# Edge sums of a graph network: the ring of gathered edge tiles with 32 places for 16, and rings of eight groups for emptied banks and first rows

## What is computed

```python
def reference(x, src, dst, ...):
    # L0: out = segment_sum(mlp(concat(x[src], x[dst])) * edge_weight, dst)
    # L1: agg = segment_sum(h[src], dst);  mean = agg / max(deg, 1)      (twice)
    # L2: out = segment_sum(h[src] * dinv[src] * dinv[dst], dst)         (twice, self loops too)
    # L3: out = segment_sum(v[src] * softmax_by_source(scores), dst)
    x = _layernorm(x + L0(x)); x = _layernorm(x + L1(x))
    x = _layernorm(x + L2(x)); x = _layernorm(x + L3(x))
```

## Time and profile before

| | us |
|---|---|
| runs | 8763.08, 8755.55, 8756.22 |
| median | 8756.22 |
| profiled execution, its own time | 8752.19 |
| its span, first to last instruction | 8750.5 |
| mean granted TensorE clock | 0.724 |

### The profile page before, as it was taken

How to read it: one execution, slowest core, us unless ns; L and a number is a source line. 1 busy time by engine, 2 the same in 40 slices (tenths; PEclk the granted TensorE clock), 3 DMA queues, 4 the chain that set the end, 5 groups by cost and what they waited for, 6 DMA issues and landing times. The chain is left out here.

```text
span 8750.5 us, 136064 instructions
## 1 busy us (share of the span) xinstructions
PE 5075.0 (58%) x26949; PEld 3942.2 (45%) x26950; DVE 4064.5 (46%) x13584; ACT 2826.8 (32%) x6967; POOL 4235.5 (48%) x4934
## 2 busy tenths in 40 slices
PE   3666667705679556965785567544444444414577
PEld 2555444504568445854564455333322233303555
DVE  3555558861222122755662227544444444452458
ACT  0544452361343124841331248311111111100239
POOL 4777750056630565036615664555555555507650
PEclk7766679955789567976896679666666666655679
DMA  1222225572358223943574458311111111122348
GB/s 31 65 66 66 67 60 173 183 242 64 93 156 248 70 85 116 337 161 101 156 230 120 118 169 288 117 49 53 47 48 49 48 48 48 48 20 61 90 149 295
DMA packets 610422, 1013.48 MB, mean 116 GB/s; under 512 B 174962, under 2 KB 177296, under 8 KB 610064
## 3 DMA queue, kind: packets, MB, share of 16 engines
q1 hardware_dynamic: 279472, 417.77, 16.1%
q10 hardware_dynamic: 197568, 359.75, 11.6%
q0 software_dynamic: 133280, 234.88, 10.9%
HBM read 648.88 MB, written 363.07 MB: 116 GB/s over the span
## 5 line engine op out<-in xcount | busy, mean ns | idle before, releaser
L447 PE MATMUL agg_bank<-agg_msgs,agg_onehot 128*128 x7840 | 1573.5, 361 | 976.0 <-issue 697.9
L447 PEld LDWEIGHTS agg_bank<-agg_msgs,agg_onehot 128*128 128x128 f32 x7840 | 1344.7, 256 | 1273.3 <-issue 1263.5
L385 DVE TENSOR_TENSOR agg_onehot<-iota,rel 128x512 f32<-128x512 f32 x1176 | 814.3, 692 | 1717.5 <-issue 630.3
L316 POOL DMA_INDIRECT agg_msgs<-y,agg_rows x784 | 784.3, 1000 | 409.3 <-issue 210.9
L1446 PE MATMUL score_look<-score_rounded,score_loT 128*128 128x392 bf16 x392 | 178.5, 455 | 716.9 <-ACT score_loT L1515 535.1
L1398 POOL DMA_INDIRECT by_source<-score_line,score_places x392 | 397.3, 1013 | 261.7 <-DVE score_line L1572 152.7
L482 ACT ACTIVATE agg_kept<-agg_bank,inv_root 128x128 f32<-128x128 f32 x784 | 226.5, 367 | 879.9 <-PE agg_bank L447 453.5
L1093 POOL DMA_INDIRECT mlp_xs<-in_x,mlp_rows x392 | 396.6, 1012 | 233.5 <-issue 152.0
L482 ACT ACTIVATE agg_kept<-agg_bank,inv_deg 128x128 f32<-128x128 f32 x784 | 224.2, 368 | 875.2 <-PE agg_bank L447 665.4
L447 PE MATMUL agg_bank<-agg_weighted,agg_onehot 128*128 x1568 | 349.5, 394 | 265.4 <-DVE agg_onehot L385 137.5
L313 POOL DMA_INDIRECT agg_weight<-weights,agg_rows x392 | 408.9, 1043 | 182.2 <-issue 111.5
(11 more groups left out here) (333 smaller groups left out, 12898.8 us busy)
## 6 DMA issues: line engine op xcount, KB each, us to landing
sums<-agg_kept ACTq DMA_DIRECT2D x588, 256.0 KB
agg_first<-y ACTq DMA_DIRECT2D x196, 256.0 KB
messages<-mlp_m SPq DMA_DIRECT2D x98, 256.0 KB
agg_first<-in_x ACTq DMA_DIRECT2D x98, 256.0 KB
agg_msgs<-messages SPq DMA_DIRECT2D x98, 256.0 KB
l_z<-sums SPq DMA_DIRECT2D x98, 256.0 KB
x<-l_o POOLq DMA_DIRECT2D x98, 256.0 KB
l1a_s<-sums SPq DMA_DIRECT2D x98, 256.0 KB
```

The source lines that it names most:

```text
L316: pool.indirect_dma_start(msgs[:, j, :], None, table[:, :], bass.IndirectOffsetOnAxis(ap=rows[:, third, j:j + 1], axis=0)).then_inc(sm[f"g ...
L385: nc.vector.tensor_tensor(onehot[:, j, :, :], k.iota[:, 0:P].unsqueeze(1).to_broadcast([P, Q, P]), k.rel[:, ds(i * (4 * Q) + j * Q, Q)].un ...
L447: t.matmul(bank[:, column[q], :], onehot[:, j, q, :], messages[:, slot[q], :], start=False, stop=True, skip_group_check=True)\
```

## The change

`RING` becomes 32, and a new constant `KEPT` = 8 sizes the rings `kept` and `first` and their semaphores, while the PSUM banks stay `BANKS` = 4. ScalarE's loop now goes over eight groups; a bank number is taken modulo 4. A bank emptied for group g is refilled for group g+4, now from place (u+4) modulo 8 of `first`, and that place is then loaded for group g+12 (before, g+8). SyncE's loop in agg0 and agg5 goes over eight groups instead of four. GpSimd's loops cover three blocks of 32 gathers.

```diff
-RING = 16
+RING = 32
 BANKS = 4
+KEPT = 8
...
-    ROUNDS = (GROUPS - 2 * BANKS) // BANKS
+    ROUNDS = (GROUPS - BANKS - KEPT) // KEPT
...
-        kept = sb("kept", [P, BANKS, Q, C])
+        kept = sb("kept", [P, KEPT, Q, C])
...
-            first = sb("first", [P, BANKS, Q, C])
+            first = sb("first", [P, KEPT, Q, C])
...
-                        if live(i, u):
+                        if live(i, u, RING // Q):
                             load(i, u)
-                        if weights is not None and live(*before_by(i, u, 2)):
-                            arrive(*before_by(i, u, 2))
-
-                    rounds(sp, body, 2 if weights is not None else 0)
+                        if weights is not None and live(*before_by(i, u, 2, RING // Q), RING // Q):
+                            arrive(*before_by(i, u, 2, RING // Q))
+
+                    rounds(sp, body, 2 if weights is not None else 0, deep=RING // Q)
...
-                    to = bank[:, u * Q:(u + 1) * Q, :]
+                    to = bank[:, u % BANKS * Q:(u % BANKS + 1) * Q, :]
...
-                    g = i * BANKS + u
+                    g = i * KEPT + u
+                    b = u % BANKS
...
+                    after_it = (u + BANKS) % KEPT
                     if not last_round or g + BANKS < GROUPS:
-                        fill(u, i + 2)
+                        fill(after_it, i + (1 if after_it > u else 2))
                     act.dma_start(rows_of(out, g), kept[:, u, :, :]).then_inc(sm[f"written{u}"], 16)
-                    if before is not None and (not last_round or g + 2 * BANKS < GROUPS):
+                    if before is not None and (not last_round or g + BANKS + KEPT < GROUPS):
                         act.wait_ge(sm["ready"], g + (BANKS + 1))
-                        load_first(g + 2 * BANKS, u)
+                        load_first(g + (BANKS + KEPT), after_it)
```

More of the change, by code:

```diff
@@ L261, in aggregate @@
     BLOCKS, REST = ET // RING, ET % RING
-    ROUNDS = (GROUPS - 2 * BANKS) // BANKS
+    ROUNDS = (GROUPS - BANKS - KEPT) // KEPT
     whole = rows_of_edges is None or weights is not None
     loads = RING // Q if whole else RING
-    sm = phase(nc, name, [f"gathered{j}" for j in range(loads)] + [f"written{u}" for u in range(BANKS)] + [f"before{u}" for u in range(BANKS)]
+    sm = phase(nc, name, [f"gathered{j}" for j in range(loads)] + [f"{s}{u}" for s in ("written", "before") for u in range(KEPT)]
                + [f"weight{u}" for u in range(RING // Q)] + ["rows", "pass_pool", "pass_dve", "arrived", "hot", "tallied", "tally_c", "tally_to_act", "tally_rooted", "tally_to_pe", "tally_offset", "onehot", "summed", "zeros", "cleared", "ready", "emptied", "weighted"])
@@ L481, in empty @@
                         if scale is not None:
-                            last = a.activation(kept[:, u, q, :], bank[:, u * Q + q, :], ACT.Copy, scale=scale[:, ds(g * Q + q, 1)])
+                            last = a.activation(kept[:, u, q, :], bank[:, b * Q + q, :], ACT.Copy, scale=scale[:, ds(g * Q + q, 1)])
                         elif q == 0:
-                            last = a.activation(kept[:, u, :, :], bank[:, u * Q:(u + 1) * Q, :], ACT.Copy)
+                            last = a.activation(kept[:, u, :, :], bank[:, b * Q:(b + 1) * Q, :], ACT.Copy)
                     last.then_inc(sm["emptied"], 1)
                     act.wait_ge(sm["emptied"], g + 1)
+                    after_it = (u + BANKS) % KEPT
                     if not last_round or g + BANKS < GROUPS:
-                        fill(u, i + 2)
+                        fill(after_it, i + (1 if after_it > u else 2))
                     act.dma_start(rows_of(out, g), kept[:, u, :, :]).then_inc(sm[f"written{u}"], 16)
-                    if before is not None and (not last_round or g + 2 * BANKS < GROUPS):
+                    if before is not None and (not last_round or g + BANKS + KEPT < GROUPS):
                         act.wait_ge(sm["ready"], g + (BANKS + 1))
-                        load_first(g + 2 * BANKS, u)
+                        load_first(g + (BANKS + KEPT), after_it)
                 if before is not None:
-                    for u in range(BANKS):
+                    for u in range(KEPT):
                         load_first(u, u)
@@ L504, in _ @@
                         act.wait_ge(sm["ready"], u + 1)
-                        load_first(u + BANKS, u)
-                for u in range(BANKS):
+                        load_first(u + KEPT, u)
+                for u in range(KEPT):
                     empty(0, u, False)
                 with act.Fori(1, ROUNDS) as i:
-                    for u in range(BANKS):
+                    for u in range(KEPT):
                         empty(i, u, False)
-                for g in range(ROUNDS * BANKS, GROUPS):
-                    empty(g // BANKS, g % BANKS, True)
+                for g in range(ROUNDS * KEPT, GROUPS):
+                    empty(g // KEPT, g % KEPT, True)
                 if tally is not None and tally[0] is k.dst_lo:
@@ L515, in _ @@
                     a.activation(k.root[:, :], k.inv_root[:, :], ACT.Sqrt).then_inc(sm["tally_rooted"], 1)
-                for u in range(BANKS):
-                    act.wait_ge(sm[f"written{u}"], 16 * len(range(u, GROUPS, BANKS)))
+                for u in range(KEPT):
+                    act.wait_ge(sm[f"written{u}"], 16 * len(range(u, GROUPS, KEPT)))
         end_phase(nc, sm)
```

## The result

The changed kernel took 8855.73 us (median of 4 runs, 8847.41 to 8865.14), the kernel before 8755.88 us on the same chip (4 runs, 8748.25 to 8763.08). The ratio is 1.0107, with a 95% interval of 1.0095 to 1.0120: 1.1% slower, and 5.7 us above the range that was forecast. The profiled execution took 8857.90 us, its span 8856.3 us, the mean granted TensorE clock 0.729 (before 0.724).

A forecast was written before the change was run, and what follows sets the result against it. It took gather phases to be bound by one account shared by gathers and other engines' instructions. Five phases at +8.7 us, all else 0, gave +44 us on 8752.19, 8796; plus 4.0 to the median, 8800 us, range 8735 to 8850.

The forecast's parts named there:

- the lag: End of each gather phase: GpSimd finishes further ahead, leaving more quads after the last gather; 8.7 us per phase, 44 in all.
- The slow stretch: Gather phases: SyncE, VectorE and TensorE step at 0.7 us until the full ring pauses GpSimd; expected fewer and longer, 20 us and more.
- the 12 to 20: Sign in the later profile: 12 to 20 one-hots remain after the last gather, instead of 7 to 9.
- agg0, `kept` and `first`, and the fewer turns: Phase without gathers, rings of eight and half as many loop turns: each taken as 0, with small possible effects.
- The first rival: Gather phases: slow stretches come at their own times, so 32 places outlast them; -250 us, 8506 us, chance 10%.
- The account: Gather phases: gathers and other engines' instructions draw on one always-spent time budget, 1.218 us per GpSimd count, 0.0202 per other count.
- still fills each window: Sign in the later profile: prices 1.218 and 0.0202 us times the counts still use up each window's time.
- I take half, 6 quads or 8.7 us per phase: End of each gather phase: 6 more quads after the last gather, between 0 and 12; 44 us over five phases.
- the full lag: Ring full at each last gather: 12 quads of 1.45 us, 17.4 us per phase, +87 us, 8843 us; up to 8864.
- The net price of a quad: Each quad done after the last gather instead of before: 1.85 us less 0.4 given back, 1.45 us.
- The gross price: Time per quad after the last gather, averaged over the earlier profile's five phase ends: 1.85 us.
- The end of a phase is not covered by anything: End of each gather phase: work left when GpSimd finishes has no gathers beside it; cost taken as 8.7 us per phase.

The follow-up runs named there:

- depth 16 in the ring of 32: The changed kernel with its 32 places, loops and buffers, but GpSimd allowed only 16 tiles ahead of TensorE; 8766.57 us, ratio 0.9998 to the kernel before.
- the lead taken back early: The changed kernel with GpSimd allowed 32 tiles ahead for the first 74 groups of gathers, 16 for the last 24; 8834.53 us, ratio 1.0081 to the kernel before.
- the added instructions: The kernel before with four unread semaphore increments behind each count in SyncE's loop in agg1 to agg4; 8829.71 us, ratio 1.0075.

## Why the prediction was wrong, and where it was right

The direction and the mechanism of the lag held; its size did not, and the time fell 5.7 us above the range.

**What held.** The ring's waits were moved, not removed: 463 us of idleness against 479. The slow stretch lasted until the larger ring was full, and its end followed the pause. First to last gather changed by -0.4 to -0.8%, and 18 to 20 one-hots were left, within the 12 to 20 that were named as the sign. GpSimd's waits at the ring in agg1 are fewer and longer only before 2300 (22 of 51.4 us, the longest 7.6, against 29 of 59.0, the longest 4.5), not behind it. agg0, `kept` and `first`, and the fewer turns were put at 0, and the 0.9992 of the ring of 16 with rings of eight and the 0.9998 of depth 16 in the ring of 32 bear that out. The first rival, ring waits that come back as time, had no part in it.

**The account.** It was named as a sign, "still fills each window", and held only roughly. Windows of agg1 after come to 94 to 96 us of 100. From first to last gather of agg1 it gives 416 x 1.218 + 3634 x 0.0202 = 580 us before and 404 x 1.218 + 3417 x 0.0202 = 561 after, 19 us less, where 2.4 us less were measured. Twelve of the counts that are gone are short row copies; charged per gather, at 1.218 x 416/392 = 1.293 us, it gives 580 and 576 for 591.3 and 588.9. Two more rows of the kernel before speak against it as a general rule, agg3 from its first to its last gather, and a window in L0's edge phase:

```profile
3821.30:4425.70 604.40, 375.05 (x1870) 277.14 (x1868) 343.53 (x935) 160.26 (x453) 400.06 (x415) 0.73 0.41 123
...
500.00:600.00 100.00, 70.16 (x350) 54.36 (x349) 55.83 (x226) 53.83 (x148) 72.08 (x86) 0.70 0.24 69
```

The windows at 2000 and 4220 were the two it was solved from, so agg3 never tested it: there 5126 counts of the others stand beside the gathers, against 3634 in agg1, and the stretch is 13 us longer, 9 ns for each and not 20. And the window of L0's edge phase has 86 counts of GpSimd (68 of them gathers) and 1073 of the others, which the account prices at 126 us of 100. The 44 us of the forecast take only 0.4 us per quad from it, which the gather stretches bore out.

**The step that failed.** It is "I take half, 6 quads or 8.7 us per phase". The runs showed 10.8 quads more per phase, nearly the 12 of the full lag that the prediction worked out itself. The reason for taking half was that it depends on where in its cycle the ring stands at the last gather. It doesn't: the five phases left 18, 18, 20, 20 and 18 one-hots. The row that decided it was on the table, the 22 waits and 39.3 us after 2300 in the earlier trace rows. A ring that stops its producer every few gathers up to the end is full at the end; the counts left over grew with the depth in each run from 12 to 32. At 1.45 us, 54 quads instead of 30 add 35 us to the 44.

**The second size.** The net price of a quad was 1.45 us and measured 96.3/54 = 1.78. What it gives back to the account was right: 20.3 us of shorter gather stretches over 54 quads are 0.38 us, against 0.4. The gross price was not: (96.3 + 20.3)/54 = 2.16 us against 1.85. The 1.85 came from tails of seven to nine quads in the earlier trace rows; the 94 one-hots now stand 179.7/89 = 2.02 us apart on average, and the kernel without gathers shows 2.04 us over a whole phase. That covers 0.17 of the 0.31 us; the rest is not traced. With the net price it adds 54 x 0.33 = 18 us, and 44 + 35 + 18 = 97 us are the 96.3 us of the five phases.

**The other steps.** "The end of a phase is not covered by anything" was too narrow, as the lead taken back early showed: with GpSimd stopped for part of the time in mid-phase the others ran at 2.3 us per quad, hardly faster than beside it (2.4 to 2.6 in the same windows before), and about two thirds of the cost stayed. The upper end was a mistake of its own: the full lag was worked out at 8843 to 8864 us, and the range was cut at 8850.

**What is shown and what is not.** Shown is that the lead costs the time (depth 16 in the ring of 32), in step with its size (24 and 32), and that it is not the buffers, the addresses or the loops. That gathers and the other engines hold each other up is shown by the kernel without gathers, less what the clock may account for. That they share one account with a price per instruction is not shown: it fits some windows and misses others, and the added instructions can be read both ways. What they share stays open. So does whether the recording of the trace has a part in it: every execution on record has a span and a clock from its trace, and none ran without one.

## What to carry to other kernels

A ring that is full at the end of a phase is a debt: its depth, less what the consumer needs to be fed, is worked off with the producer standing. The debt is made early, while the producer runs ahead and the consumer is slow; at the end it is only paid. Before deepening one, look at whether the producer still waits on it near the end; if so, count the consumer's steps per place and charge all of them at the consumer's own pace. And ask whether a full ring is the cause of the wait or the result of something that slows the consumer; here the best depth measured was 12, below the 16 places of the kernel before, and 8 starved.

## What was not expected of the hardware

- While gathers stream, TensorE's sequencer steps at 0.7 us for up to 37 us on end, SyncE's and VectorE's for parts of it (SyncE's for 18 us), and they recover only after GpSimd has paused some 5 us (1991.5 to 1997). Without gathers agg1 had no such stretch.
- 6144 semaphore increments of 17 ns on an engine that mostly waits cost 65 us, 10.6 ns each.
- 392 gathers at a free 1.24 us (486 us) and other work of 410 us, on different engines, take 613.6 us side by side.
